# Self-attention block: key-major scores with a separate maximum pass, changed to query-major scores whose float16 probabilities are transposed by DMA

## The reference, cut to what matters

```python
B, H, W, C = 16, 32, 32, 512             # 1024 tokens a batch, 8 heads of 64
x = ft.reshape(B, N, C)
qkv = x @ w_qkv + b_qkv
q, k, v = jnp.split(qkv.reshape(B, N, N_HEADS, 3 * D_HEAD), 3, axis=-1)
attn = jnp.einsum('bxhd,byhd->bxyh', q, k) * SCALE
attn = jax.nn.softmax(attn, axis=2)
res = jnp.einsum('bxyh,byhd->bxhd', attn, v)
res = res.reshape(B, N, N_HEADS * D_HEAD) @ w_out + b_out + x
```

## Time and profile before

| | |
|---|---|
| median of 2 runs | 4104.32 us (4103.62 to 4105.03) |
| profiled execution | 4103.61 us, its span 4101.8 us |
| one batch in mid-run | 253.5 and 254.1 us |
| one head in mid-batch (8 steps) | 24.5 us |
| granted TensorE clock | 1.00 of full speed in every stretch |
| busy: PE, PEld, DVE, ACT, POOL | 95%, 76%, 66%, 66%, 43% |

### The profile page before, as it was taken

One profiled execution on the slowest core, in us unless ns is written; L12 is line 12 of the kernel. 1 busy time (PEld: TensorE's weight loads), 2 busy tenths in 40 slices (PEclk: granted clock), 3 DMA queues, 4 the chain that ended last, 5 costly groups with the idle time before them and its releaser, 6 DMA issues.

```text
span 4101.8 us, 105442 instructions
## 1 busy us (share of the span) xinstructions
PE 3915.1 (95%) x38156; PEld 3113.8 (76%) x38156; DVE 2721.0 (66%) x4395; ACT 2707.0 (66%) x2965; POOL 1769.3 (43%) x888
## 2 busy tenths in 40 slices
PE   6999999999999999999999999999999999999999
PEld 5777777777777777777777777777777777777777
DVE  5757757577575775757667576675766757667576
ACT  4756847568475774757757477574775747657476
POOL 1534525345253552535525255352553525435254
PEclk9999999999999999999999999999999999999999
DMA  3011021110202102020021211202011121110201
GB/s 98 22 54 42 20 76 25 57 39 17 79 22 70 26 20 76 22 74 22 25 71 24 71 24 28 68 22 73 22 37 58 25 71 25 38 58 22 63 22 43
DMA packets 100845, 179.85 MB, mean 44 GB/s; under 512 B 16192, under 2 KB 16192, under 8 KB 100288
## 3 DMA queue, kind: packets, MB, share of 16 engines
q1 hardware_dynamic: 100288, 172.29, 14.9%
HBM read 71.57 MB, written 33.55 MB: 26 GB/s over the span
## 4 chain that ended last, share of the span: by engine, by line
PE 68%; DVE 17%; issue 11%; ACT 1%; DVEq 1%; POOL 1%; DMA 0%; SPq 0%; ACTq 0%; POOLq 0%
PE psum L472 31%; PE psum L503 9%; PE psum L532 6%; PE psum L534 6%; DVE max_parts L749 6%; PE psum L556 4%; PE psum L560 4%; PE psum L558 4%; DVE q_shift L728 3%; DVE k_lo_hi L726 3%; DVE p_lo L771 2%; PE psum L486 2%; DVE q_shift L762 2%; ACT p_hi L655 1%; POOL p_lo L380 1%
## 5 line engine op out<-in xcount | busy, mean ns | idle before, releaser
L380 POOL TENSOR_TENSOR p_lo<-p_full,p_hi 128x1024 f16<-128x1024 f32 x752 | 1607.3, 2143 | 2069.7 <-ACT p_hi L655 2069.7
L749 DVE TENSOR_REDUCE max_parts<-psum 128x1 f32<-128x512 f32 x2048 | 1341.3, 686 | 516.7 <-PE psum L503 507.8
L654 ACT ACTIVATE p_full<-psum,prob_bias 128x1024 f32<-128x1024 f32 x1024 | 1144.1, 1117 | 384.8 <-PE psum L534 371.1
L655 ACT ACTIVATE p_hi<-psum,prob_bias 128x1024 f16<-128x1024 f32 x1024 | 1137.2, 1111 | 0.0
L556 PEld LDWEIGHTS psum<-v_parts,p_hi 128*128 128x128 f16 x8192 | 743.8, 98 | 263.2 <-issue 161.8
L556 PE MATMUL psum<-v_parts,p_hi 128*128 128x65 f16 x8192 | 857.2, 193 | 35.5 <-DVE o_heads L781 19.9
L558 PE MATMUL psum<-v_parts,p_hi 128*128 128x64 f16 x8192 | 850.7, 192 | 0.0
L560 PE MATMUL psum<-v_parts,p_lo 128*128 128x65 f16 x8192 | 848.0, 194 | 0.0
L532 PE MATMUL psum<-q_hi_hi,k_lo_hi 128*128 128x512 f32 x2048 | 818.7, 400 | 1.9
L503 PE MATMUL psum<-k_lo_hi,q_hi_hi 128*128 128x512 f32 x2048 | 769.3, 429 | 51.7 <-DVE q_shift L728 21.5
L534 PE MATMUL psum<-q_shift,k_shift 128*128 128x512 f32 x2048 | 802.3, 392 | 0.0
(11 more groups left out here) (61 smaller groups left out, 4269.8 us busy)
## 6 DMA issues: line engine op xcount, KB each, us to landing
x_in<-in_x SPq DMA_DIRECT2D x128, 256.0 KB, 3.9
k_shift<-k_lo_hi SPq DMA_DIRECT2D x256, 128.0 KB, 2.2
q_hi_hi<-q_hi_hi SPq DMA_DIRECT2D x256, 128.0 KB, 2.3
y_tile<-in_x SPq DMA_DIRECT2D x128, 256.0 KB, 2.8
result<-y_tile SPq DMA_DIRECT2D x128, 256.0 KB, 2.8
o_heads<-in_L_conv_w_qkv SPq DMA_DIRECT2D x12, 256.0 KB, 4.1
o_heads<-in_L_conv_w_out SPq DMA_DIRECT2D x4, 256.0 KB, 4.1
out_bias<-in_L_conv_b_out SPq DMA_DIRECT2D x1, 256.0 KB, 5.8
```

The source lines that it names most:

```text
L380: nc.gpsimd.tensor_tensor(p_lo[:, s % P_SLOTS, :, :], p_full[:, s % 2, :, :], p_hi[:, s % P_SLOTS, :, :], ALU.subtract).then_inc(p_lo_read ...
L654: nc.scalar.activation(p_full[:, s % 2, :, :], score_banks(s), ACT.Exp, scale=SCALE, bias=prob_bias[:, :])
L655: nc.scalar.activation(p_hi[:, s % P_SLOTS, :, :], score_banks(s), ACT.Exp, scale=SCALE, bias=prob_bias[:, :]).then_inc(exp_done, 1)
L749: nc.vector.reduce_max(max_parts[:, u % 2, q_tile, k_half:k_half + 1], max_bank(w), AX.X).then_inc(max_tile_done, 1)
```

## The change

Scores are computed with the **queries on the partitions**: a step is now one tile of 128 queries against all 1024 keys, still 64 a batch and 8 a head. DVE reads each row's maximum off the score tile itself, makes the bias of the exponential from it, and ACT applies it. The whole pass for the maxima (L503, L749, L755, L510, L762, the copies into `k_shift`) goes. But the probabilities now have the wrong side on the partitions for the product with V, so SP issues, for each step, two DMA transposes in the crossbar, 128x1024 float16 each: p_hi into `pT_hi`, p_lo into `pT_lo`. There are three buffers for p_hi and p_lo (as before), four for their transposes, and in slot s PE does the scores of s+1, a part of a fill, and the product with V of `s - LAG`, that is of s-4 and not s-1.

```diff
+LAG = 4
+P_SLOTS = 3
+T_SLOTS = 4
+QK_PARTS = {0: (0, 0, 4), 1: (0, 4, 8), 2: (0, 8, TERMS), 3: (1, 0, 4), 4: (1, 4, 8), 5: (1, 8, TERMS)}
-POOL_STEPS = (0, 2, 3, 4, 6, 7)
+DVE_STEPS = (1, 5)
...
+        def transposed(engine, i, s):
+
+            engine.wait_ge(pT_ready[s % T_SLOTS], signals_led(i, STEPS // T_SLOTS * 32, 32 * (s // T_SLOTS + 1)))
+
+        def slot_of_p_free(engine, i, s):
+
+
+            for t in range(s - P_SLOTS, s - P_SLOTS + 1) if s >= P_SLOTS else range(-P_SLOTS, 0):
+                transposed(engine, i, t)
...
         @block.sync
...
+                def transpose_hi(s):
+                    sp.wait_ge(p_hi_ready, signals_led(i, STEPS, s + 1))
+                    sp.wait_ge(pv_done, signals_led(i, STEPS, max(s + 1 - T_SLOTS, 0)))
+                    sp.dma_start_transpose(pT_hi[:, s % T_SLOTS, :, :], p_hi[:, s % P_SLOTS, :]).then_inc(pT_ready[s % T_SLOTS], 16)
+
+                def transpose_lo(s):
+                    low_part_ready(sp, i, s)
+                    sp.dma_start_transpose(pT_lo[:, s % T_SLOTS, :, :], p_lo[:, s % P_SLOTS, :]).then_inc(pT_ready[s % T_SLOTS], 16)
...
+                for s in range(STEPS + 1):
+                    if s < STEPS:
+                        transpose_hi(s)
+                    if s > 0:
+                        transpose_lo(s - 1)
+                    if s % TOKEN_TILES == 6 and s // TOKEN_TILES + 1 < HEADS:
+                        q_to_lower_rows(s // TOKEN_TILES + 1)
...
-            with sp.Fori(0, BATCH - 1) as i:
-                batch(i, False)
-            batch(BATCH - 1, True)
+            for i in range(BATCH):
+                batch(i, i == BATCH - 1)
...
         @block.tensor
...
                 def step_scores(s):
...
+                    if t % UNIT == 0:
+                        pe.wait_ge(q_hi_hi_ready[t // UNIT], signals(i, HEADS * 16, (h + 1) * 16))
+
                     pe.wait_ge(exp_done, signals_led(i, STEPS, max(s - 1, 0)))
...
+                        nc.tensor.matmul(score_banks(s)[:, half, :], q_hi_hi[:, h % 2, toks], k_lo_hi[:, h % 2, keys],
                                          start=True, stop=False)
...
+                        last = nc.tensor.matmul(score_banks(s)[:, half, :], q_zero_lo[:, h % 2, toks],
+                                                k_lo_hi[:, h % 2, keys], start=False, stop=True)
                     last.then_inc(scores_ready, 1)
...
+                    transposed(pe, i, s)
+                    for kt in range(TOKEN_TILES):
+                        hi, lo = pT_hi[:, s % T_SLOTS, kt, :], pT_lo[:, s % T_SLOTS, kt, :]
...
                 for s in SLOTS:
...
                     if 0 <= s + 1 < STEPS:
                         step_scores(s + 1)
...
+                    for part in fills_of_slot(s):
+                        fill(*part)
+                    if 0 <= s - LAG < STEPS:
+                        step_pv(s - LAG)
...
                 def exp_step(s):
...
+                    act.wait_ge(row_bias_ready, signals(i, STEPS, s + 1))
+                    slot_of_p_free(act, i, s)
+                    scores = score_banks(s).rearrange("p b k -> p (b k)")
+                    bias = row_bias[:, s % 2:s % 2 + 1]
+                    nc.scalar.activation(p_hi[:, s % P_SLOTS, :], scores, ACT.Exp, scale=SCALE, bias=bias).then_inc(p_hi_ready, 1)
+
+                    if s >= 2:
+                        low_part_ready(act, i, s - 2)
+                    nc.scalar.activation(p_full[:, s % 2, :], scores, ACT.Exp, scale=SCALE, bias=bias).then_inc(exp_done, 1)
...
+                def step_max(s):
+                    dve.wait_ge(scores_ready, signals(i, STEPS, s + 1))
+                    nc.vector.reduce_max(row_max[:, s % 2:s % 2 + 1], score_banks(s).rearrange("p b k -> p (b k)"),
+                                         AX.X).then_inc(max_ready, 1)
+                    dve.wait_ge(max_ready, signals(i, STEPS, s + 1))
+                    nc.vector.tensor_scalar(row_bias[:, s % 2:s % 2 + 1], row_max[:, s % 2:s % 2 + 1], -SCALE, PROB_BIAS,
+                                            ALU.mult, ALU.add).then_inc(row_bias_ready, 1)
...
                 for s in SLOTS:
...
+                    if 0 <= s + 1 < STEPS:
+                        step_max(s + 1)
+                    for w in completed_in_slot(s):
+                        take(w)
                     if 0 <= s < STEPS and not on_pool(s):
                         step_lo(s)
```

More of the change, by code:

```diff
@@ L43 @@
[L43 to L50, removed]
-        return []
[L52 to L59, removed]
@@ L62 @@
[L62 to L81, removed]
+PV_BANKS = (4, 5)
@@ L84, in completed_in_slot, with fills_of_slot @@
+FILL_BANKS = (6, 7)
+TERMS = 3 * CH_TILES
+SLOTS = range(-1, STEPS + LAG + 1)
+QK_PARTS = {0: (0, 0, 4), 1: (0, 4, 8), 2: (0, 8, TERMS), 3: (1, 0, 4), 4: (1, 4, 8), 5: (1, 8, TERMS)}
+def fills_of_slot(s):
+    head, at = divmod(s, TOKEN_TILES)
+    if not 0 <= s < STEPS or head + 1 == HEADS or at not in QK_PARTS:
+        return []
+    half, first, last = QK_PARTS[at]
+    return [(("qk", head + 1, half), first, last)]
 def completed_in_slot(s):
     return [w for w, _, last in fills_of_slot(s) if last == TERMS]
-def is_first_half(w):
-    return w[0] == "qk" and w[2] == 0
@@ L93, in consumed_in_slot @@
[L93 to L106, removed]
 def named(*names):
-    kinds = {"T": ("x_transpose",), "V": ("v",), "Q": ("qk", 0)}
+    kinds = {"T": ("x_transpose",), "V": ("v",), "Q": ("qk", 0), "O": ("o_transpose",), "Y": ("project",)}
@@ L112, in named @@
     return [(*kinds[name[0]], int(name[1])) for name in names]
[L116 to L125, removed]
@@ L294, in _ @@
                 sp.sem_inc(y_stored[k])
+            for k in range(T_SLOTS):
+                sp.sem_inc(pT_ready[k])
             w_view = w_qkv.rearrange("(c p) n -> p c n", p=P)
@@ L533, in step_scores @@
+                    for half in range(HALVES):
+                        keys = slice(half * HALF, (half + 1) * HALF)
+                        nc.tensor.matmul(score_banks(s)[:, half, :], q_hi_hi[:, h % 2, toks], k_lo_hi[:, h % 2, keys],
                                          start=True, stop=False)
-                        last = nc.tensor.matmul(score_banks(s)[:, n, :], k_shift[:, h % 2, keys],
-                                                q_shift[:, h % 2, cols], start=False, stop=True)
+                        last = nc.tensor.matmul(score_banks(s)[:, half, :], q_zero_lo[:, h % 2, toks],
+                                                k_lo_hi[:, h % 2, keys], start=False, stop=True)
@@ L550, in step_pv @@
-                    for n in range(KEYS_PER_STEP):
-                        kt = key_tile(s, n)
-                        for qt in range(Q_TILES):
-                            qs = slice(qt * P, (qt + 1) * P)
-                            hi, lo = p_hi[:, s % P_SLOTS, n, qs], p_lo[:, s % P_SLOTS, n, qs]
-                            nc.tensor.matmul(pv[:, qt, :], hi, v_parts[:, kt, h, DIM:DIM + PV_W],
-                                             start=kt == 0 and qt == 0, stop=False, skip_group_check=True)
-                            nc.tensor.matmul(pv[:, qt, 0:DIM], hi, v_parts[:, kt, h, 0:DIM],
-                                             start=False, stop=False, skip_group_check=True)
-                            last = nc.tensor.matmul(pv[:, qt, :], lo, v_parts[:, kt, h, DIM:DIM + PV_W],
-                                                    start=False, stop=kt == TOKEN_TILES - 1, skip_group_check=True)
+                    h = s // TOKEN_TILES
@@ new lines, in step_pv @@
+                    u, t = divmod(s, UNIT)
+                    pv = pv_bank(u)
+                    if t == 0:
+                        pe.wait_ge(o_ready, signals_led(i, UNITS, max(u - 1, 0)))
+                    transposed(pe, i, s)
+                    for kt in range(TOKEN_TILES):
+                        hi, lo = pT_hi[:, s % T_SLOTS, kt, :], pT_lo[:, s % T_SLOTS, kt, :]
+                        nc.tensor.matmul(pv[:, t, :], hi, v_parts[:, kt, h, DIM:DIM + PV_W],
+                                         start=kt == 0 and t == 0, stop=False, skip_group_check=True)
+                        nc.tensor.matmul(pv[:, t, 0:DIM], hi, v_parts[:, kt, h, 0:DIM],
+                                         start=False, stop=False, skip_group_check=True)
+                        last = nc.tensor.matmul(pv[:, t, :], lo, v_parts[:, kt, h, DIM:DIM + PV_W],
+                                                start=False, stop=kt == TOKEN_TILES - 1, skip_group_check=True)
@@ L662, in _ @@
                         exp_step(s)
-                    for part in high_parts_in_slot(s):
-                        take_hi(*part)
+                    for w in completed_in_slot(s):
+                        take_hi(w)
                 for w in AFTER:
```

306 lines of the change are left out of this document (84 added, 222 removed).

## The result

| | before | after |
|---|---|---|
| median of 2 runs | 4104.32 us | 5338.1 us (5336.56 to 5339.65) |
| ratio, 95% interval | | 1.3006 [1.295, 1.3062] |
| one batch in mid-run | 253.8 us | 330.7 us |
| one head in mid-batch | 24.5 us | 33.1 us (mean of six) |
| mean granted clock | 1.00 | 0.893 |

The change makes the kernel 30% slower. The forecast, 4975 us, had the direction, and is short by 363 us; its range, 4000 to 9000 us, was wide enough to hold a small gain as well. As before, a sum by stages closes: 16 x (8 x 33.1 + 66) + 42 = 5335 us.

A forecast was written before the change was run, and what follows sets the result against it. The prediction took a ring of waits through the transposes, no full engine, as the bound: 29.8 us a head, 70 us for the rest of a batch, 16 x (8 x 29.8 + 70) + 42 = 4976, rounded to 4975 us; range 4000 to 9000.

The forecast's parts named there:

- P: Time from SP's issue of hi(s) to the landing of lo(s-1): 1.8 + 2c and 0.1 hand-over, 5.4 us.
- the ring: Loop of waits PE, DVE, ACT, POOL or DVE, SP, DMA, PE; a head takes 19.0 + 2P, 29.8 us.
- c: Time for which one transpose keeps the DMA queue: taken as 1.75 us.
- its signs: PE share some 75%, idle ahead of products and scores, ACT waiting for pT_lo, heads 27 to 31 us.
- The forecast's own case: Whole kernel bound by the ring with c between 1.0 and 1.9: 4590 to 5050 us, chance 0.45.
- the queue-bound case: DMA queue bounds when c exceeds 1.9; a head costs 16c, total above 5050 us, chance 0.28.
- Step 1: At a head's start: scores 0.9, product with V of 8h-5 0.8, hand-over 0.3; 2.0 us.
- step 8: At a head's end: SP issues lo(8h+5), 0.6, then Q's copy, 2.3 to landing, and 0.1; 3.0 us.
- step 4: PE in mid-head: scores, fill and product twice, 5.2, and 0.3 hand-over; 5.5 us.
- The queue bounds: Rival for the DMA queue: each block its own DMA, c = 3.7, total 8740 us; queue-bound chance 0.28.
- PE stays the bound: Rival: the ring is slack, a head is 20.3 us, total 3760 us; faster by over 2% had chance 0.13.
- The transposes hide, the ring doesn't: Rival: with P = 0 another path of waits leaves about 25 us a head, total 4360 us; no separate chance given.

The follow-up runs named there:

- both edits: Q's copies issued early in halves and LAG = 3 in place of 4, against the changed kernel: 4593.76 us (ratio 1.1195).
- e3: Next head's Q copied in halves at steps 4 and 7, not both at step 6, against the changed kernel: 4834.74 us (ratio 1.1782).

## Why the prediction was right in direction and short in size

The prediction's eight steps, read off the head shown above (2516.81 to 2549.88, 33.07 us, which is the mean head), from the first scores to the next head's:

| step | forecast | measured | from, to |
|---|---|---|---|
| 1 scores, product, hand-over | 2.0 | 3.5 | 2516.81, SP 2520.30 |
| 2 P | 5.4 | 5.35 | 2520.30, ACT 2525.65 |
| 3 exp(8h+1) | 2.2 | 2.2 | 2525.65, PE 2527.82 |
| 4 two slots of PE | 5.5 | 6.2 | 2527.82, SP 2534.00 |
| 5 P | 5.4 | 5.2 | 2534.00, ACT 2539.23 |
| 6 exp(8h+5), high parts | 3.5 | 3.4 | 2539.23, 2542.64 |
| 7 low parts, p_lo | 2.8 | 2.8 | 2542.64, 2545.42 |
| 8 lo(8h+5), then Q's copy | 3.0 | 4.5 | 2545.42, PE 2549.88 |
| sum | 29.8 | 33.1 | |

**Right.** The mechanism: the exponentials wait for the transposes of three steps before, lo(s-1) waits behind hi(s), and Q's copy behind both. Moving Q's copy and shortening the ring gave 503 (with the clock's rise) and 456 us with no work removed. P came out at 5.2 to 5.35 us against 5.4, the maximum at 1.22 us as priced, the rest of a batch at 66 against 70. c was taken as 1.75 and is 1.38 by itself, 1.51 in the kernel: inside the stated 1.0 to 1.9, so the ring and not the queue bounds, as forecast. That P fits with a smaller c is luck of two errors. With c = 1.51 the formula, 1.8 + 2c + 0.1, gives 4.9 us. The trace has 2.15 us from SP's issue of hi to that of lo (2520.30 to 2522.45), a time of SP that the formula lacks, and 3.2 us from there to the exponential.

**What of its signs held.** PE's share fell to 72%, ACT waits for pT_lo, and PE waits for Q's copy ahead of a head's first scores. But PE hardly waits ahead of the product with V (86 us in 47 waits), heads are 33.1 us and not 27 to 31, and transposes land after 3.2 to 3.3 us and not 3.5 to 5.5. The forecast's own case, a ring with c between 1.0 and 1.9, ended at 5050 us. By its list, 5338 us belongs to the queue-bound case, and that isn't what happened: c lay inside its bounds, and three other terms of the ring were too small.

**The steps that failed.** First, "the granted clock is 1.00 in every stretch, so it needs no term". It was read from a kernel whose PE is busy for 24.1 of 24.5 us; this one rests 6 us at each change of head and comes back at 0.50. Step 1 is 1.5 us longer by it: the four score matmuls take 1.87 us until the product with V starts at 2518.68, not 0.9, and the product 1.35, not 0.8. Junk on PE regained 137 us, 1.2 us for each of 112 changes of head. Second, "An SP issue I take at 0.6 us", from a copy's row. A transpose costs SP 1.23 to 1.34 us. In step 8, hi(8h+6) still keeps SP until 2545.84 and lo(8h+5) takes 1.34 us: 1.5 us longer, together with a copy that lands after 2.5 us and not 2.3. No experiment made SP's issue cheaper alone, so that this is SP's time is read from the timeline, and shown by e3 only in so far as Q's place in the queue matters. Third, 0.7 us in step 4: between its two slots PE waits 0.37 us for an exponential (2531.05) that had itself waited 1.11 us for a transpose (2528.88), and the first score matmul of each slot takes 0.34 us and not 0.23. I had counted the two slots as PE's work without a gap. 1.5 + 0.7 + 1.5 - 0.4 = 3.3 us a head; with 4 us less for the rest of a batch that is 16 x (8 x 3.3 - 4) = 358 of the 363 us.

The trace also shows a second path of nearly the same length through steps 6 to 8: SP's hi(8h+5), released by the product of 8h+1 at 2541.86, and the three transposes behind it. It ends at the same copy, 0.5 us later than the low part alone would allow. Where two paths tie, removing one gives less than its length.

**The rivals.** "The queue bounds" is false for the kernel as changed (share 66.9%) and true for it once the ring is short (1.00 with both edits), at far less than the 8740 us it was priced with: each block isn't handled alone. "PE stays the bound" is false. "The transposes hide, the ring doesn't" had the ring without them at 25 us a head: measured 24.0 to 25.6 with Q early and a lag of three, and 26.2 without these, where the clock falls as well (0.904, and (4516.68 - 42) / 16 = 280 = 8 x 26.2 + 70). Its total of 4360 lies between the two, 4232 and 4517.

## What to carry to other kernels

When a change makes the path of a tile longer, draw the whole loop of waits before adding up engines: buffers that come free late and the order of one issuing queue are links of it, and a longer lag can make it longer. Copies that don't depend on the new transfers belong ahead of them in a queue; here that place was worth 503 us, the part of the clock included. For a tile like this one (256 KB within SBUF), price a transposing DMA at about twice the plain copy in queue time (1.38 against 0.69 us) and at 1.2 us of its issuer. And where a change leaves PE idle for some 6 us, as here, price the work behind the gap at half the clock, too.

## What the runs showed of the hardware

- A DMA transpose of 128x1024 float16 within SBUF: 1.38 us of queue at 190 GB/s, 3.3 us from issue to landing, 3.08 us a piece when one waits for the other; the plain copy 0.69 us at 382 GB/s and 2.3 us to landing in the kernel.
- SP's time to issue it, 1.23 us, against 0.47 us for the copy of the same 256 KB. In the kernel that only moves data an issue (median 1.33 us) takes nearly as long as a transpose keeps the queue (1.38), so which of the two sets that rate can't be told.
- Its queue time isn't the same everywhere: 1.38 us by itself (share 1.00) and in the kernel with half the transposes, 1.51 in the changed kernel, (0.809 x 4592.0 - 479) / 2048 = 1.58 with both edits. A full queue alone doesn't make it longer; what does isn't shown.
- TensorE's granted clock fell from 1.00 to 0.50 during 6 us without work, and the work after it ran at 0.50 for at least 5.5 us in one head and for 3.4 us in the next.
